# Attention plus quantized FFN in one kernel: denominators as one block per batch row, a new order of the FFN banks, and all orders written out

## The reference

```python
x = x + xattn(layernorm(x), ctx, ctx, Wq, Wk, Wv, Wo)
x = x + ffn(layernorm(x), w_gate, w_up, w_down, their scales, inv_gate, inv_up, inv_inter)

# xattn: 32 query heads of 32, 8 key/value heads (4 query heads share one)
probs = softmax(q @ k.T * 32**-0.5);  out = (probs @ v) @ Wo
# ffn: per row of x (bfloat16): q = round(x * inv / scale), scale = max|x * inv| / 127
gate, up = quant_gemm(w_gate), quant_gemm(w_up)          # 1024 -> 512
inter = clip(silu(gate) * up, -10, 10);  out = quant_gemm(quant(inter), w_down)  # 512 -> 1024
```

## Time and profile before

| | |
|---|---|
| median of 3 runs | 772.9 us (771.8 to 775.0) |
| profiled execution, its own time | 774.1 us |
| profiled execution, its span | 772.4 us |
| PE, DVE, ACT, POOL busy | 689.4, 579.4, 269.8, 210.8 us |
| mean granted TensorE clock | 0.964 of 2.4 GHz |

### The profile page before, as it was taken

The page is one execution under the profiler, slowest core; times in us unless marked ns, Lnnn a source line. Parts: engine busy times, 40 slices in busy tenths (PEclk is TensorE's granted clock), DMA queues, the critical chain, the costliest instruction groups (busy, mean ns, idle before and its releaser), DMA issues.

```text
span 772.4 us, 13682 instructions
## 1 busy us (share of the span) xinstructions
PE 689.4 (89%) x5072; PEld 427.2 (55%) x5072; DVE 579.4 (75%) x820; ACT 269.8 (35%) x417; POOL 210.8 (27%) x170
## 2 busy tenths in 40 slices
PE   4999998888989999999999999999999999579843
PEld 3888885563467446744664466446655654233321
DVE  5544344745888789988998899899889986886663
ACT  4443124371334133514351525052505340433131
POOL 3521330001332333133313240414132322232341
PEclk9999999898999999999999999999999999988986
DMA  8766384776022602260226022503250313210100
GB/s 316 246 239 197 118 225 139 222 245 207 2 52 90 195 2 52 91 193 1 51 89 193 1 69 77 187 1 79 105 150 2 84 65 124 58 63 1 55 28 27
DMA packets 40482, 83.85 MB, mean 109 GB/s; under 512 B 4848, under 2 KB 19184, under 8 KB 40432
## 3 DMA queue, kind: packets, MB, share of 16 engines
q1 hardware_dynamic: 38144, 74.99, 31.7%
q0 software_dynamic: 2304, 8.39, 2.7%
HBM read 62.26 MB, written 21.10 MB: 108 GB/s over the span
## 4 chain that ended last, share of the span: by engine, by line
PE 63%; DMA 14%; DVE 11%; ACT 4%; issue 4%; SPq 3%; POOL 0%; POOLq 0%; DVEq 0%; ACTq 0%
PE bank L619 15%; PE bank L546 15%; PE bank L655 5%; PE bank L508 5%; DMA k_stack<-k_dram 4%; PE bank L521 4%; PE bank_s L565 4%; PE bank L677 4%; DMA q_stack<-q_dram 3%; PE bank_o L595 3%; PE bank_d L599 3%; DVE o_norm L1355 3%; DMA q_dram<-q_st_lo 3%; PE bank_s L583 2%; SPq L353 2%
## 5 line engine op out<-in xcount | busy, mean ns | idle before, releaser
L546 PE MATMUL bank<-act_t_hi,wq_hi 128*128 128x256 f16 x512 | 140.3, 274 | 0.0
L546 PE MATMUL bank<-act_t_hi,wq_lo 128*128 128x256 f16 x512 | 140.1, 274 | 0.0
L546 PE MATMUL bank<-act_t_lo,wq_hi 128*128 128x256 f16 x512 | 140.1, 274 | 0.0
L1355 DVE RECIPROCAL o_norm<-bank_d 128x512 f32<-128x512 f32 x32 | 107.3, 3352 | 16.3 <-PE bank_d L599 16.3
L1346 DVE TENSOR_REDUCE neg_max<-bank_s 128x4 f16<-128x512 f32 x128 | 84.9, 686 | 35.1 <-PE bank_s L565 34.9
L619 PE MATMUL bank<-wo_hi,o_t_hi 128*128 128x512 f16 x256 | 97.5, 381 | 0.8 <-POOL o_t_lo L1707 0.8
L619 PE MATMUL bank<-wo_lo,o_t_hi 128*128 128x512 f16 x256 | 97.2, 380 | 0.0
L619 PE MATMUL bank<-wo_hi,o_t_lo 128*128 128x512 f16 x256 | 97.0, 379 | 0.0
L1707 POOL TENSOR_TENSOR o_t_lo<-o_norm,o_t_hi 128x512 f16<-128x512 f32 x32 | 37.6, 1176 | 217.3 <-ACT o_t_hi L1043 217.3
L1029 ACT ACTIVATE probs<-bank_s 128x512 f32<-128x512 f32 x128 | 73.8, 601 | 36.6 <-PE bank_s L583 34.2
L565 PE MATMUL bank_s<-k_stack,q_stack 96*128 96x128 f16 x512 | 46.9, 223 | 18.5 <-issue 8.6
(11 more groups left out here) (121 smaller groups left out, 1245.8 us busy)
## 6 DMA issues: line engine op xcount, KB each, us to landing
q_stack<-q_dram SPq DMA_DIRECT2D x48, 256.0 KB, 4.8
inp<-in_x SPq DMA_DIRECT2D x16, 512.0 KB, 4.5
x<-in_x SPq DMA_DIRECT2D x16, 512.0 KB, 4.0
out<-x POOLq DMA_DIRECT2D x16, 512.0 KB, 3.0
q_dram<-q_st_hi SPq DMA_DIRECT2D x8, 512.0 KB, 2.7
q_dram<-q_st_lo SPq DMA_DIRECT2D x8, 512.0 KB, 3.8
w_gate<-in_ctx_t SPq DMA_DIRECT2D x6, 512.0 KB, 5.6
w_up<-in_ctx_t SPq DMA_DIRECT2D x6, 512.0 KB, 6.7
```

Source lines behind the costliest of these rows:

```text
L546: ins = nc.tensor.matmul(bank[:, :, jj, :], wq_sb[a][:, 2 * item + jj, kc, :], act_t[m][:, kc, :, :], start=(kc == 0 and (a, m) == PARTS[0 ...
L1355: nc.vector.reciprocal(o_norm[:, :], bank_d[:, :]).then_inc(recip_done, 1)
```

## The change

Four things change together.

1. **Denominators.** `bank_d` is filled by 16 matmuls of 128 columns for each `pv` (4 query heads x 4 groups of 32 rows) instead of 4 of 512. The weights are a window of `head_sel` in which one column is ones, so that the 32 denominators of a row and their 128 tokens end up as one 128 x 128 block for each batch row, accumulated over both `pv`. One `RECIPROCAL` of 128 x 128 for each row (`recip`) writes `r_sb`; `save_r` sends it to DRAM (64 KB), and `fill_r` reads it back with each row repeated over the 32 head rows (128 x 1024 float32, 512 KB). ScalarE copies `bank_o` to SBUF (`o_out_`), which frees the bank for the next `pv`, and `norm` is one product of two SBUF tensors on VectorE. GpSimd's `o_lo` and ScalarE's `o_hi_` stay.
2. **Bank order.** `bank3` goes row by row: the output product of row `r`, then the down product of row `r-2`, then gate and up of row `r-1`.
3. **Buffers.** Attention outputs of odd pairs go to the place of the key weights, so `o_hi_` waits for the output product of three rows before instead of one; `x2` has three buffers (the third in `kv_st`); the value weights' place holds `o_raw` and the reciprocals.
4. **Orders.** The loop is gone; each engine's whole order is written out. The output product of pair 0 and the queries of pair 2 now begin while the last weight pieces are still being loaded.

The core of the diff:

```diff
+def place3(r, name):
+
+    if name in W3:
+        return N3 * r + W3.index(name)
+    if name in T3:
+        return N3 * (r + 2) + len(W3) + T3.index(name)
+    return N3 * (r + 1) + len(W3 + T3) + G3.index(name)
...
+        o_odd = {h: flat(wk_sb[h]).rearrange("p (b t j n) -> p b t j n", b=2, t=NT, j=REP) for h in ("hi", "lo")}
...
+            def save_r(p, b):
+                r = 2 * p + b
+                sp.wait_ge(recip_done, r + 1)
+                sp.dma_start(r_dram[r], r_sb[:, :]).then_inc(r_saved, 16)
+
+            def fill_r(p, b):
+                r = 2 * p + b
+                if needed(2 * r):
+                    sp.wait_ge(o_split, 2 * r)
+                if p == 1 and b == 0:
+                    sp.wait_ge(kv_full, NKV1 * PAIRS)
+                sp.wait_ge(r_saved, 16 * (r + 1))
+                halves = ((0, 1), (1, 2)) if is_first(p) else ((0, 2),)
+                for t0, t1 in halves:
+                    rows = r_dram[r].rearrange("(g c) n -> g c n", g=4)[:, REP * t0:REP * t1, :]
+                    rows = rows.rearrange("g c n -> g (c n)").unsqueeze(1).broadcast_to([4, HD, (t1 - t0) * REP * P])
+                    sp.dma_start(r_rows(p, t0, t1), rows).then_inc(r_filled, 16)
...
                 if needed(2 * r + t):
-                    pe.wait_ge(norm_done, 2 * r + t)
+                    pe.wait_ge(o_out, 2 * r + t)
+                if t == 0 and needed(r - 1):
+                    pe.wait_ge(recip_done, r - 1)
...
-                for g in range(4):
-                    rows = slice(HD * g, HD * g + HD)
-                    ins = nc.tensor.matmul(bank_d[rows, :], ones32[:, :], probs[:, g, :],
-                                           start=True, stop=True, tile_position=(0, HD * g))
+                for j in range(REP):
+                    c0 = (NKV - (REP * t + j)) % NKV
+                    for g in range(4):
+                        ins = nc.tensor.matmul(bank_d[HD * g:HD * g + HD, b * P:(b + 1) * P], head_sel[:, c0:c0 + HD],
+                                               probs[:, g, j * P:(j + 1) * P], start=(t == 0 and j == 0),
+                                               stop=(t == NT - 1 and j == REP - 1), tile_position=(0, HD * g))
...
+            def o_out_(p, b, t):
+                r = 2 * p + b
+                act.wait_ge(pv_full, 2 * r + t + 1)
+                if needed(r):
+                    act.wait_ge(o_split, 2 * r + t - 1)
...
+                nc.scalar.copy(o_raw(p, t), bank_o[:, :]).then_inc(o_out, 1)
...
+            def recip(p, b):
...
+                nc.vector.reciprocal(r_sb[:, :], bank_d[:, b * P:(b + 1) * P]).then_inc(recip_done, 1)
+
             def norm(p, b, t):
...
-                nc.vector.reciprocal(o_norm[:, :], bank_d[:, :]).then_inc(recip_done, 1)
-                dve.wait_ge(recip_done, 2 * r + t + 1)
-                nc.vector.tensor_tensor(o_norm[:, :], bank_o[:, :], o_norm[:, :], ALU.mult).then_inc(norm_done, 1)
+                dve.wait_ge(o_out, 2 * r + t + 1)
+                dve.wait_ge(r_filled, r_filled_by(p, b))
+                nc.vector.tensor_tensor(o_raw(p, t), o_raw(p, t), r_rows(p, t, t + 1), ALU.mult).then_inc(norm_done, 1)
```

More of the change, by code:

```diff
@@ L147, in build @@
         x_loaded = [sem(f"x_loaded{b}") for b in range(2)]
-        res_loaded = [sem(f"res_loaded{b}") for b in range(2)]
+        res_loaded = [sem(f"res_loaded{i}") for i in range(3)]
         ctx_hi = sem("ctx_hi")
@@ L207, in needed @@
         def needed(value):
[L209 to L214, removed]
+            return value > 0
         def is_first(p):
[L217 to L225, removed]
+            return p == 0
         def pieces(dram, dst, n):
@@ new lines, in _ @@
+            save_r(1, 1)
+            fill_r(1, 1)
+            save_max(2, 0)
+            fill_v(2, 0)
+            fill_max(2, 0)
+            fill_q(2, 1)
+            fill_k(2, 1)
+            load_x(5, 0)
+            load_res(1, 1)
+            save_max(2, 1)
+            save_r(2, 0)
+            load_x(5, 1)
+            fill_max(2, 1)
+            spill_q(3)
+            fill_r(2, 0)
+            fill_v(2, 1)
+            fill_q(3, 0)
+            fill_k(3, 0)
+            save_r(2, 1)
@@ new lines, in _ @@
+            fill_r(2, 1)
+            load_res(2, 0)
+            fill_v(3, 0)
+            save_max(3, 0)
+            fill_max(3, 0)
+            spill_q(4)
+            fill_q(3, 1)
+            fill_k(3, 1)
+            load_res(2, 1)
+            save_r(3, 0)
+            load_x(6, 1)
+            save_max(3, 1)
+            fill_v(3, 1)
+            fill_r(3, 0)
+            fill_max(3, 1)
+            load_x(6, 0)
+            fill_q(4, 0)
+            fill_k(4, 0)
+            save_r(3, 1)
@@ new lines, in _ @@
+            fill_max(6, 0)
+            fill_v(6, 0)
+            fill_r(5, 1)
+            fill_q(6, 1)
+            fill_k(6, 1)
+            fill_v(6, 1)
+            save_max(6, 1)
+            save_r(6, 0)
+            fill_max(6, 1)
+            fill_r(6, 0)
+            load_res(5, 1)
+            spill_q(7)
+            fill_q(7, 0)
+            fill_k(7, 0)
+            save_max(7, 0)
+            fill_v(7, 0)
+            save_r(6, 1)
+            fill_max(7, 0)
+            fill_r(6, 1)
@@ L480, in _ @@
+            load_res(6, 0)
+            fill_q(7, 1)
+            fill_k(7, 1)
+            save_r(7, 0)
+            fill_v(7, 1)
+            fill_r(7, 0)
+            load_res(6, 1)
+            save_max(7, 1)
+            fill_max(7, 1)
+            load_res(7, 0)
+            save_r(7, 1)
+            fill_r(7, 1)
+            load_res(7, 1)
             for b in range(2):
@@ L985, in _ @@
-            run(pe, start, steady, finish)
+            pe.wait_ge(consts_ready, 11)
+            xt(0, 0, 0)
+            xt(0, 0, 1)
+            k(0, 0)
+            k(0, 1)
+            v(0, 0)
+            v(0, 1)
+            xt(0, 1, 0)
+            xt(0, 1, 1)
+            k(1, 0)
+            k(1, 1)
+            q(0, 0, 0)
+            v(1, 0)
+            q(0, 0, 1)
+            q(0, 0, 2)
+            v(1, 1)
+            q(0, 0, 3)
+            k(2, 0)
+            q(0, 1, 0)
+            q(0, 1, 1)
@@ L1297, in _ @@
+            qt(7, 1, 2)
         @block.vector
@@ L1795, in _ @@
-            run(pool, start, steady, finish)
+            rstd1_(0, 0)
+            ctx(0, 0)
+            ctx(0, 1)
+            rstd1_(0, 1)
+            ctx(1, 0)
+            ctx(1, 1)
+            ctx(2, 0)
+            rstd1_(1, 0)
+            ctx(2, 1)
+            ctx(3, 0)
+            ctx(3, 1)
+            ctx(4, 0)
+            ctx(4, 1)
+            rstd1_(1, 1)
+            ctx(5, 0)
+            ctx(5, 1)
+            ctx(6, 0)
+            ctx(6, 1)
+            ctx(7, 0)
+            ctx(7, 1)
```

3034 lines of the change are left out of this document (2052 added, 982 removed).

## The result

The changed kernel took 782.8 us (779.0 to 786.5, 4 runs) against 773.4 us before (771.8 to 775.0, 4 runs): a ratio of 1.012, with a 95% interval of 1.006 to 1.018. It is slower, by more than the 0.5% that a measurement of this kernel tells from no change; 755 us had been forecast, with a range of 730 to 774. The profiled execution took 780.7 us, its span is 778.8.

What follows compares the result with a forecast made beforehand. The prediction took TensorE to bound the loop (437 of 454 us busy). Its terms, -17.8 - 0.8 - 10.9 + 2.5 + 5.8 + 4.2 = -17.0 on a span of 772.4, gave 755.4; it said 755 us, range 730 to 774.

Steps and rivals of the forecast that it cites:

- `fill_r` stands ahead of `fill_max`: SyncE's queue, rows (3,1) and (4,1): the small transfer lands behind 512 KB, 2.1 us lost twice, +4.2, bounds 0 and +20.
- The fourth rival: Fill of the reciprocals: outermost dimension 4, so only four DMA engines carry it, 6.4 us instead of 1.6; +19, 774 us; 12%.
- Weights stretch: While the last weight pieces load, other TensorE work lies beside them: a loss of 7 us instead of 24.8, -17.8.
- The third rival: Weights stretch: pieces pace themselves through three slots, stretching to 70 us, so extra TensorE work only fills the wait; 773 us; 10%.
- Loop and finish: Loop: a wait between `ti` and `dn` goes, key and query fills cost, -0.8; finish: 15 us lost instead of 25.9, -10.9.
- Tail: After the last output product, `quant(7,0,1)` now follows `ti`, a copy and `dn` of row (6,1): +2.5, bounds 0 and +5.
- Narrow denominators: Each `pv`: denominators by 128-column matmuls, `bank_d` 1.04 us from first to last start against 0.86; +5.8 in all.
- VectorE's 94 us at nothing: Shorter reciprocals relieve VectorE of 94 us, costed by itself at nothing, since TensorE's work covers VectorE in the loop.
- The first rival: Nearly gapless: only TensorE binds, relieved VectorE lets kept waits vanish, no price for narrow matmuls or fills; 726 us; 22%.

Runs made afterwards that it cites:

- the version with four fills: Changed kernel with each fill of reciprocals issued as four transfers, one for each group of 32 partitions, instead of one: 738.1 us, ratio to before 0.958.
- Experiment 8: Kernel before, with ScalarE doing `exp(0,1,7)` ahead of the hi halves of the last two weight pieces instead of behind them: 771.9 us, ratio 0.9997.
- experiment 4: Kernel before, with each block of denominators filled by 16 matmuls of 128 columns instead of 4 of 512: 772.1 us, ratio 1.0001.
- experiment 9: Kernel before, with each reciprocal taken of 128 columns instead of 512 and used for all four heads (three scaled wrongly): 771.3 us, ratio 1.0007.
- experiment 6: The version with four fills, with each 128x128 reciprocal done seven times, giving VectorE back 91 us: 835.9 us, ratio to the kernel before 1.082.

## Why the prediction was wrong

I set the time lost on TensorE (span less the 650.2 us that all its work takes at the starts of the earlier trace rows) beside the prediction's terms, up to 180.3 us, from there to the end of the last output product, and in the tail. The work done by 180.3 us is counted from the matmuls in the trace as in the prediction: 143.9 us of it before, 156.3 after, 162.5 in the version with four fills. The tail holds 12.6 us of work before and 14.6 in the other two; what is left belongs to the middle.

```
                      before    four fills    after
up to 180.3 us         36.4        17.8        24.0
to the last wo_        55.3        35.5        71.7
tail                   30.5        32.7        32.9
sum = span - 650.2    122.2        86.0       128.6
```

**The step that failed** is the term "`fill_r` stands ahead of `fill_max`": +4.2 us, with bounds 0 and +20. It measured +42.6 on the profiles (128.6 - 86.0), 45 on the medians, 42 by the ratios. Two things in it were wrong. The landing was taken from a broadcast load of 512 KB, 6.3 us, whose rows are spread over 128 partitions one by one; that row was near in size and not in shape, and the fill took 9.4. And only the two rows where `fill_max` is directly behind it were counted. In the trace `st` waits for the maxima 8 times and VectorE for the reciprocals 12 times, and stores of maxima in SyncE's queue land late as well. TensorE is idle for 31.1 us more than with four fills (91.6 against 60.5 us; `st`'s waits for the maxima alone are 19.1 of them), and the other 11.5 us are slower matmuls: 687.2 us busy against 675.7, at a granted clock of 0.97 against 0.98.

All terms together, as measured in the table: -18.6 up to 180.3 us, -19.8 in the middle, +2.2 in the tail, 0 for the narrow matmuls and +42.6 for the fills are the +6.4 us between the spans. That the time is only 28 us above the forecast, with 38 too little for the fills, is luck: the middle gave 8 us more than the sum had, and the price of the narrow matmuls was not paid.

**The fourth rival** had the mechanism and the rule, at 12%. Its size was wrong in the same two ways: 6.4 us for a landing of 9.4, and four rows for a dozen, so 19 us where 42.6 were lost. With its 774 at the edge of the range the range missed too.

**Weights stretch**, -17.8: right. 18.6 us come back by 180.3 us in the version with four fills, 12.4 in the change as it was made. Experiment 8 agrees that it is other work for TensorE and not the place of one `exp`. The third rival falls.

**Loop and finish**, -0.8 and -10.9: right in sign, short in size, 19.8 instead of 11.7. The sum had kept 6.4 us of waits for the fills of `k_stack` and `q_stack` in the loop and 2.9 + 3.4 in the finish; over the whole span of that version `s` waits 8.1 us for `k_stack` and not once for `q_stack`'s rows from `q_dram`. Which of the parts, written-out order or banks, gave this was not tried apart.

**Tail**, +2.5: from the end of the last output product to the end of the span it is 47.3 us with four fills and 47.5 after, against 43.1: +4.2. 2.0 of these are products that had been done earlier, so the loss grew by 2.2.

**Narrow denominators**, +5.8: nothing (experiment 4). The starts within a `pv` are 0.87 / 32 = 0.027 us apart, with each its own weight load of 0.11 us. The Trainium skill's figure of about 25 ns as the least distance between starts (TensorE: Matmul & The Clock Gate, "Back-to-back issue gap") gave 0 for this term, and the trace agrees.

**VectorE's 94 us at nothing:** true of the kernel before, to within 0.3% (experiment 9), and wrong as a statement about the change. In the new order 91 us more on VectorE cost 98, 98, 98 and 84 us in four arrangements (738.1 to 835.9, 784.4 to 882.5, 755.4 to 853.2, 756.0 to 840.2; by the ratios 96, 99, 96 and 81), with VectorE busy for 70% of the span at most. VectorE isn't full, so I read it as the written order following VectorE's queue so closely that most of what delays VectorE delays TensorE. So the change is one thing and not two: short reciprocals alone give nothing (experiment 9), and the new order with 91 us more at the reciprocals is slower than before by 8% (experiment 6). Two things are mixed in that 8%, which no run here takes apart: the repeats hold VectorE's queue, and they make each row's reciprocals 5.7 us late. Only two places in VectorE's queue were tried.

**The first rival** (nearly gapless, 726) is what the version with four fills approaches, at 738, 12 us above it and 17 below my 755. For the change as it was made it was wrong, as its 726 has nothing for the fills.

## What to carry to other kernels

Before a broadcast or reshaping DMA is priced, look at the outermost dimension of its two sides, not only at its bytes: one transfer of 512 KB for each row, over four groups, cost 42 to 45 us of a kernel of 783, and the same bytes cut into four transfers over 32 rows each were hidden. A slow transfer is to be priced by everything issued behind it on that queue, and by the clock, which had fallen after the stall of 5.3 us shown above. And an order written out by hand around a freed engine can use that engine's slack up: here the saving was worth nothing before the reordering, and giving it back cost nearly its whole length after it, so test either with the other in place.

## What the runs showed of the hardware

A small transfer issued behind a slow large one took up to the large one's time: the 8 KB store of the maxima landed in 1.4 us at best and 7.7 at worst, its fill in up to 9.3. One fill with an outermost dimension of 4 kept a quarter of the DMA engines' time busy (share 0.25, 96 GB/s). Two issued one behind the other, with an outermost dimension of 2 each, kept an eighth busy between them (0.12, early and late), and the second landed after 13.1 to 14.3 us. After 5.3 us without work TensorE ran at 1.2 GHz for some 3 us; over the kernel slower matmuls were about a quarter of what the fills cost (11.5 of 42.6 us). Narrow float32 matmuls on a quarter of the rows each, 128 columns wide, ran at the rate of wide ones.
